# Row maxima over pairs of PSUM banks: two VectorE reductions per attention unit in place of four

## What is computed

```python
energy = jnp.einsum('bhsk,bhtk->bhst', Q, K)                       # masked, causal where asked
score = jax.nn.softmax(energy / jnp.sqrt(dk), axis=-1)
out = jnp.einsum('bhst,bhtk->bhsk', score, V)
```

## Time and profile before

| what | value |
|---|---|
| median of 3 runs | 1673.72 us (1671.73 to 1675.11) |
| profiled execution, first to last instruction | 1673.8 us |
| TensorE (PE) busy | 1616.5 us (97%) |
| VectorE (DVE) busy | 1387.1 us (83%) |
| ScalarE (ACT) busy | 1039.8 us (62%) |
| GpSimd (POOL) busy | 493.3 us (29%) |
| granted TensorE clock, mean | 0.990 of full speed |

### The profile page before, as it was taken

The page is one execution under the profiler, slowest core; times in us unless marked ns, Lnnn a source line. Parts: engine busy times, 40 slices in busy tenths (PEclk is TensorE's granted clock), DMA queues, the critical chain, the costliest instruction groups (busy, mean ns, idle before and its releaser), DMA issues.

```text
span 1673.8 us, 61139 instructions
## 1 busy us (share of the span) xinstructions
PE 1616.5 (97%) x25060; PEld 1393.2 (83%) x25060; DVE 1387.1 (83%) x3585; ACT 1039.8 (62%) x2667; POOL 493.3 (29%) x1256
## 2 busy tenths in 40 slices
PE   7899999999999999999999999999999999999986
PEld 6777888888888888888888888888888888888774
DVE  4689888888888889888888988888898888898652
ACT  2355666766666676666667666666766666676652
POOL 2333223333322332332233233223323322333110
PEclk9999999999999999999999999999999999999997
DMA  6110000000000000000000000000000000000000
GB/s 216 52 64 21 6 18 31 18 25 28 22 3 24 25 24 24 25 17 9 24 25 25 25 24 22 5 24 25 24 25 24 17 10 24 21 28 19 5 5 7
DMA packets 31316, 44.37 MB, mean 27 GB/s; under 512 B 3008, under 2 KB 26176, under 8 KB 30912
## 3 DMA queue, kind: packets, MB, share of 16 engines
q1 hardware_dynamic: 31040, 40.45, 7.4%
HBM read 36.12 MB, written 4.33 MB: 24 GB/s over the span
## 4 chain that ended last, share of the span: by engine, by line
PE 55%; DVE 36%; issue 5%; POOL 2%; DMA 1%; ACT 1%; SPq 0%; DVEq 0%; POOLq 0%; ACTq 0%
PE ring L639 18%; PE ring L645 14%; PE ring L627 6%; DVE conv L1358 5%; DVE maxima_at L1258 5%; PE score L707 4%; DVE decay L1392 4%; PE score L731 3%; PE ring L773 3%; DVE decay L1396 2%; PE ring L858 2%; DVE conv L1364 2%; DVE QB L1269 2%; DVE conv L1353 2%; PE score L671 2%
## 5 line engine op out<-in xcount | busy, mean ns | idle before, releaser
L1533 POOL TENSOR_TENSOR stat<-stat 128x1 f32<-128x1 f32 x224 | 131.7, 594 | 617.2 <-DVE stat L1224 616.6
L1019 ACT COPY actT<-ring 128x256 f32<-128x256 f32 x256 | 95.5, 373 | 291.7 <-PE ring L627 290.5
L1258 DVE TENSOR_REDUCE maxima_at<-score 128x4 f32<-128x512 f32 x388 | 240.8, 684 | 25.5 <-PE score L707 24.5
L1052 ACT ACTIVATE weights<-score 128x512 f32<-128x512 f32 x388 | 200.7, 607 | 28.5 <-PE score L731 27.9
L1358 DVE SCALAR_TENSOR_TENSOR conv<-raw,vectors,conv 128x128 f32<-128x128 f32 x576 | 169.0, 349 | 6.8
L639 PE MATMUL ring<-actT,w_q 128*128 128x128 f32 x1024 | 141.5, 281 | 0.7 <-ACT actT L1019 0.7
L639 PEld LDWEIGHTS ring<-actT,w_q 128*128 128x128 f32 x1024 | 124.5, 191 | 12.8 <-issue 11.3
L639 PE MATMUL ring<-actT,w_up 128*128 128x128 f32 x1024 | 129.6, 281 | 0.5 <-ACT actT L1019 0.5
L639 PEld LDWEIGHTS ring<-actT,w_up 128*128 128x128 f32 x1024 | 121.1, 194 | 3.7 <-ACT actT L1019 1.1
L1184 ACT ACTIVATE gT<-ring,vectors 128x128 f32<-128x128 f32 x256 | 73.0, 368 | 72.2 <-PE ring L639 71.5
L645 PE MATMUL ring<-w_down,gT 128*128 128x256 f32 x512 | 115.9, 379 | 1.3 <-issue 1.3
(11 more groups left out here) (179 smaller groups left out, 3814.8 us busy)
## 6 DMA issues: line engine op xcount, KB each, us to landing
decay<-rates_out SPq DMA_DIRECT2D x32, 512.0 KB, 3.9
cT<-in_ctxT SPq DMA_DIRECT2D x32, 128.0 KB, 2.2
x_in<-in_x SPq DMA_DIRECT2D x32, 128.0 KB, 2.4
out<-result SPq DMA_DIRECT2D x32, 128.0 KB, 2.1
row_all<-in_rows SPq DMA_DIRECT2D x1, 1420.0 KB, 9.9
w_in<-in_in_proj SPq DMA_DIRECT2D x1, 1288.0 KB, 7.2
w_k<-in_k SPq DMA_DIRECT2D x4, 256.0 KB, 5.8
w_v<-in_v SPq DMA_DIRECT2D x4, 256.0 KB, 5.7
```

What stands on the lines that cost most here:

```text
L1019: nc.scalar.copy(dst.rearrange("p c k -> p (c k)"), t[:, 0:n]).then_inc(read, 1)
L1052: run(weights[:, turned_buffer(it, a_, l), r, :], score[:, r, :], ACT.Exp).then_inc(S["exps"], 1)
L1258: nc.vector.tensor_reduce(maxima_at[:, maxima_buffer(it, a_, l), :, 32 * r:32 * r + 17:16], score[:, r, :].rearrange("p (c f k) -> p c f k ...
L1533: tt(stat[:, l, 10:11], stat[:, l, 2:3], stat[:, l, 4:5], ALU.pow).then_inc(S[done], 1)
```

## The change

Two banks are reduced by one instruction: the input is 128x1024 (two banks), the output 128x8, in the same places of `maxima_at`. Each reduction stands behind the semaphores of both of its banks and adds 2 to `maxima`, so that all counts stay as they were. Nothing else is touched, and the orders of all engines are kept.

```diff
-                for r in range(TILES):
-                    dve.wait_ge(S[f"scores{r}"], nth_unit(it, "quads", a_, l))
+                for r in range(0, TILES, 2):
+                    for bank_of in (r, r + 1):
+                        dve.wait_ge(S[f"scores{bank_of}"], nth_unit(it, "quads", a_, l))
                     nc.vector.tensor_reduce(
-                        maxima_at[:, maxima_buffer(it, a_, l), :, 32 * r:32 * r + 17:16],
-                        score[:, r, :].rearrange("p (c f k) -> p c f k", c=DC, f=2),
-                        AX_X, ALU.max, negate=True).then_inc(S["maxima"], 1)
+                        maxima_at[:, maxima_buffer(it, a_, l), :, :].rearrange("p c (r f s) -> p r c f s", r=TILES, f=2)[:, r:r + 2, :, :, 0],
+                        score[:, r:r + 2, :].rearrange("p r (c f k) -> p r c f k", c=DC, f=2),
+                        AX_X, ALU.max, negate=True).then_inc(S["maxima"], 2)
```

## The result

| | before | after |
|---|---|---|
| median of 15 runs each, in turn on one chip | 1673.72 us (1671.73 to 1676.14) | 1678.13 us (1673.86 to 1681.45) |
| ratio | | 1.0026, 95% interval 1.0018 to 1.0033 |
| profiled execution, span | 1673.8 us | 1678.2 us |

The change is slower, by 0.26% or 4.4 us. A run's time is its span and 1.8 us around it (after's run of 1673.86 us has a span of 1672.0), so the profiled execution of before was a run of 1675.6 and that of after one of 1680.0; both lie on the slow side of their medians, by about the same. Lines of after stand one further down than those of before from L1259 on.

A forecast was written before the change was run, and what follows sets the result against it. TensorE (97% busy) and VectorE (83%) hand the kernel's end back and forth. Attention 3's -0.3 us and -0.4 us from three visible transpose waits give -0.7: span 1673.8 to 1673.1, median 1673.0 us; range 1668.7 to 1678.0.

The forecast's parts named there:

- The saving per unit, 0.134 us: VectorE's maxima units: two reductions of 1024 columns take 2.35 us in place of 2.49 for four, 0.134 us less each.
- rival 1: VectorE's reductions: each removed one saves its full latency, 0.30 us less a unit, faster at 1668.7 us; chance 0.08.
- rival 3: First reduction of attention 3: the wait costs and nothing is saved, slower, 1677.3 us or in a large form 1708; chance 0.13.
- The added wait, 0.124 us: Where VectorE waits for scores, the unit starts later by 0.034 us for bank 1 plus 0.09 behind two semaphores.
- the queue's step: A step of VectorE's queue between the scores and a reduction behind two semaphores; start 0.12 us after the matmul, not 0.03.
- Attention 3, -0.01 us a period: The maxima unit on the path: -0.134 + 0.124 = -0.01 us, 29 times, -0.3 us.
- Attentions 2 and 4, nothing: Maxima units: 2 ends 0.13 us earlier but TensorE comes 0.67 us later anyway; 4 ends as before; both gain nothing.
- The banks' later release: Bank 0 freed after 1.22 us instead of 0.68, bank 2 0.4 us later; covered by TensorE's other work, costing nothing.
- Sum: The prediction's paragraph adding up the effects at attentions 3, 2 and 4, visible waits and tail: together -0.7 us.
- rival 3's small form: Two reductions take as long as four, so 0.124 us stays at attention 3, 29 times: 3.6 us slower, 1677.3 us.

## Why the prediction was wrong

It said no difference, 1673.0 us, up to 1678.0 at the edge of the range; it is 1678.13, and slower.

- **The saving per unit, 0.134 us: right.** 2.356 against 2.486 us, 0.130. The reduction of 1024 columns takes 1220 ns against the 1.22 us forecast. The unit's full latency is not saved (rival 1), and it isn't lost either (rival 3, which needed 1.28 us). Measured, each removed instruction saves 65 ns. The Trainium skill, page "VectorE: DVE Perf Modes", section "The TRN2 errata", speaks of sources in SBUF and gives its formula for a float32 add, while these reductions read PSUM. The formula's estimates for a single instruction, 691 and 1224 ns, are near the 684 and 1220 measured; carried over to a saving of 157 ns for each removed one, as in the prediction, it doesn't agree with the traces, because neighbours overlap.
- **The added wait, 0.124 us: right, in its sum and in its parts.** Measured 0.14 = 0.04 for the second bank and 0.10 for the queue's step; the text had 0.034 and 0.09. (It divided the 1.10 us of the earlier trace rows by 32, where the row counts 29 matmuls: 0.038.) What wasn't foreseen is that a pair behind one semaphore has the step too: the version with one wait was expected to gain 0.10 us a unit and had 0.02.
- **Attention 3, -0.01 us a period: right but for 0.02 us.** 0.428 + 2.356 is 0.01 more than 0.288 + 2.486, and a period is 0.02 longer. That a delay there arrives in full is shown by the four reductions behind paired waits (0.11 us a period).
- **Attentions 2 and 4, nothing through semaphores: right**, as the timeline shows. The banks' later release: nothing, also right (bank 2's is 0.47 us by the text's own numbers, 2.35 less 0.60 + 0.60 + 0.684, and not 0.4). The transposes in front of which TensorE waits visibly come 4 times in place of 5, 3.9 us in place of 4.3. VectorE's busy time was forecast at 1374 and is 1377.7: the maxima's own fell by 12.4 us (240.8 to 228.4), that of the other instructions rose by 3.
- **The step that failed** is the one under *Sum* that gives attention 2 "nothing", and with it the silent one, that TensorE's work costs what it did because its instructions are the same. Changing attention 2 alone costs 0.31%, with four gaps and 28 periods 4.9 us longer. The path leads not over a semaphore that TensorE waits for but over the stream of TensorE's instructions: with attention 2's units changed, certain packets begin some 100 to 200 instructions later, and in the densest stretch of the period TensorE uses up what it has. None of the rivals had this mechanism; rival 3 had the sign and, by accident, the size (1677.3).
- **The range** ended just beyond rival 3's small form, and left no room for a loss of some us from a cause that the page hadn't named. Before's own trace gave little warning: its page has the 202 packets of instructions, and the idle time in front of TensorE's loads of L731 that is put down to "issue", 16.6 us, is 73 gaps of at most 0.4 us.

What stays open is how the packet's time depends on VectorE. Over the 50 us up to the late packet at 692.4 TensorE's weight loads stand at the same times in both kernels, to 0.02 us. That what a semaphore says at the moment at which TensorE's sequencer reads ahead decides how early it asks for the next packet is a guess, and no run tried it. It fits with the values that packets 50, 106 and 162 take (186 to 190, or 352 to 398), and with where they lie: 16 of the 20 late ones begin within 0.12 us of the queue step, instruction 353 or 354, in which TensorE waits for `maxima` ahead of L671. Nor is it shown why attention 2 and not 4 does it; the later release of bank 0 (0.54 us) and the count of `maxima`, which goes up by two, go with the new loop in both. The four reductions with paired waits have neither and lose packets 50, 106 and 162 all the same (though not 48, 104 and 160), so these two can't be the whole cause, and neither can the 0.13 us by which attention 2 ends earlier, which that version doesn't have.

## What to carry to other kernels

Where an engine that bounds the kernel has stretches of very short instructions (here 258 in 2.4 us), its instructions' own arrival is a resource: look in the page at the queue of instructions, and in the timeline for gaps that wait for "issue" in the midst of one line's work. A change of a tenth of a us on another engine, or some instructions more at the head, came with 0.2 to 0.3% of the time here; so test a small edit with the borders shifted too (some empty instructions at the head, in both versions) before its loss or gain is put down to the edit. And split an added wait into the later completion and the queue's own step by the semaphore events and the queue rows of the trace: by the start times alone the second bank would seem to come 0.11 us later, and it comes 0.04 later.

## What was not expected of the hardware

- TensorE ran out of instructions: gaps of 1.0 to 2.1 us (from one weight load's start to the next) in the midst of 32-row matmuls or right behind them, 35 times in 14 of 18 traces, and every time after the same count of instructions, 449 or 450 from 256 times the packet's number. A packet of 256 took 0.9 to 1.5 us.
- A gap of 1.93 us was followed by some 3.4 us at a granted clock of 0.50, and cost 3.46 us in all; gaps of 1.36 and 1.82 us cost 1.27 and 1.32. Of 35 gaps 8 had such a stretch behind them.
- When a packet was asked for took one of two values at the same instruction of the same stream: 690.8 or 692.4 us, with TensorE's weight loads of the 50 us ahead at the same times, to 0.02 us.
- Of two banks finished by matmuls in a row, started 0.007 us apart, the second's semaphore went up 0.042 to 0.043 us after the first's. A queue step in front of a reduction of VectorE added 0.07 us behind one semaphore and 0.10 behind two.
- A reduction over 128x1024 in two banks took 1220 ns, two in a row 2.36 us.
